# Narrow cross-attention: context and weights loaded in the normalization ahead of it, a second set of parts buffers, one block less up front, keys asked for in another order

## Chip, cores and metric

One core of one Trainium2 chip runs the whole program. The metric is the device time of one execution in microseconds (us), lower is better.

## What is computed

The reference is a two-layer perceiver: x is 4 batches x 256 queries x 256 features, the context 4 batches x 4096 keys x 256 features. It adds to x, one after the other: cross-attention with 16 heads of 64, self-attention, a gated mixture of 8 experts, cross-attention with 16 heads of 16 ("narrow"), differential self-attention, and a mixture of 32 experts. The change touches the narrow cross-attention and the normalization ahead of its query projection:

```
x = x + xattn(layernorm(x), ctx, ctx, lens)
# xattn: q = split(queries @ Wq); k = split(keys @ Wk); v = split(values @ Wv)     16 heads of 16
#        scores = q k^T / sqrt(16); scores = where(arange(4096) < lens, scores, -1e6)
#        out = softmax(scores) v;   return out @ Wo
```

## The kernel before

`perceiver` (L2627) runs one stage after the other. A stage is a `nc.Block()`: every engine has its own program in it, and no engine leaves before all of them have ended. For the narrow attention there are three such stages in a row: `normalize_and_transpose` (L59), `project_queries` (L147) and `narrow_attention` (L859).

**Narrow attention.** The context stands in DRAM (`ctx_split`) already split into a high and a low part, in 32 blocks (4 batches x CG = 8 blocks of 512 keys), 1 MB each. For a block n, TensorE (PE) projects keys, 2 x 6 matmuls of 512 columns into the banks `ps_s` (`project_keys`, L1080), and, for the blocks below 8, values, 2 halves x 12 matmuls of 256 columns (`project_values`, L1094), all of them with weights split into `w_high` and `w_low`. VectorE (DVE) masks the keys into `k_masked[m]` (`mask_keys`, L1278), ScalarE (ACT) copies them to `k_high[m]` (`take_high`, L1218), GpSimd (POOL) overwrites `k_masked[m]` by the low part (`take_low`, L1362), and SyncE's DMA queue (SP) stores both to the scratch rows `k_rows` in DRAM (`store_keys`, L985 and L987). ACT also copies the values out (`take_values`, L1228). m counts the two halves of the 256 features. There is one `k_masked` and one `k_high` for each m, so block n's mask waits for the landed store of block n-1.

Work then goes by pairs of heads, G = 32 of them, 8 to a batch. A pair's keys come back from `k_rows` and `edges` in 16 DMAs, 8 for either half of the keys (`load_keys`, L1000 and L1004), its queries in 6 (`load_queries`, L1014). First the row maximum is taken in ST = 16 units (`maximum`, L1112 on PE, `take_maximum`, L1291 on DVE, two banks in turn), turned and put into q (`turn_maximum` L1120, `take_maximum` L1242 on ACT). Then come 16 steps of scores (L1132), exponents (L1236) and weighting with the values (L1146). During pair a the units of pair a+1 and the projection of one later block of keys (a + FIRST) and values (a + 8) are put in by hand.

**What comes before pair 0** ("the first batch"): FIRST = CG + 3 = 11 blocks of keys and 8 of values in a ring over four `ctx` buffers, with the 16 units of pair 0 spread over it (two at each block from 5 on, the last four behind it). The order on each engine is written out by hand; each queue is in order:

- SP: both weights (L1026), ctx 0, the constants (L1028 to L1032), ctx 1 to 3, two selectors (L1035, L1036), queries 0 and 1, edges 0; then for each block its four stores, the ctx four blocks on, edges at 2, 4, 6, and the keys of pair 0 at blocks 3 (first half) and 7 (second half); behind the ring ctx 11, the value ctx 8, and the keys of pair 1.
- PE waits for the selectors, `fixed` (DVE has cleared the bank `ps_o`), `q_fixed` and both weight splits before its first matmul. The halves of the values go to `ps_m[1]` and `ps_p` for n < 4, both to `ps_p` from n = 4 on.
- POOL: 52 semaphores of the stage are raised by one (`Scope.sem`), then memsets of the queries (L1375, L1370), the two `w_low` (L1381), a memset of `v_all` (L1383) for which ACT's first `take_high` waits, then `take_low`.
- DVE: memset of `ps_o` (L1315), two `w_high` (L1271), lens and ends, edges 0 (L1284), then the masks.

## Time and profile before

| | us |
|---|---|
| median of 3 runs (4218.68 to 4230.01) | 4223.78 |
| the profiled execution | 4229.75 |
| its span, first to last instruction | 4227.9 |
| experts' last DVE instruction to the normalization's first | 2593.55 to 2594.86 |
| first weight DMA of the narrow stage | 2626.01 |
| its first matmul | 2647.57 |
| first exponent of pair 0 | 2740.16 |
| maxima of pair 1 finished | 2774.55 |
| busy over the span | PE 88%, DVE 63%, ACT 58%, POOL 39% |

Times are microseconds from the span's start. In the timeline a row is: start, length, engine, line, operation, tile written <- tiles read, shape, number of instructions merged, and in brackets the engine's idle time ahead of it with what ended it. A matmul's end is modelled, so busy TensorE time overlaps from one row to the next. "SPq" rows are DMA issues: their length is the issue, not the transfer.

### The profile page before, as it was taken

The numbers are of one execution on the slowest core, as the hardware profiler recorded it, in microseconds if no ns is written. First come the engines' busy times: TensorE is split into PE (matmuls) and PEld (weight loads), VectorE is DVE, ScalarE is ACT, GpSimd is POOL, SyncE is SP. The second block draws the span as 40 slices with busy tenths as digits, with TensorE's granted clock in tenths as the row PEclk, the third lists the DMA queues.
The fourth block names the chain that finished last, engine by engine and source line by source line (L and its number), as shares of the span: only waits on it lengthen the run. The fifth ranks groups of instructions, "written<-read, shape, count | busy, mean of one in ns | idle before, by whom it ended". The sixth has DMA issues, their size and how long they took to land. (4 is left out here: it accounts for less than half of the span.)

```text
span 4227.9 us, 77561 instructions
## 1 busy us (share of the span) xinstructions
PE 3717.0 (88%) x28216; PEld 2620.7 (62%) x28216; DVE 2669.3 (63%) x3564; ACT 2458.3 (58%) x4550; POOL 1650.8 (39%) x1365
## 2 busy tenths in 40 slices
PE   5899999999999999999777895699999987767299
PEld 2677777777777777777454794555555543333298
DVE  4766666666666666666155412477877877457577
ACT  3577777777777777777424111266666666435165
POOL 1566666666666666666402201201111000014033
PEclk9999999999999999999788897899999999779599
DMA  5776777677767776665110384777887754000011
GB/s 194 274 251 245 252 255 256 244 252 259 248 242 260 256 246 225 231 223 203 62 34 8 141 320 154 243 162 178 177 166 178 154 81 66 19 11 1 15 48 43
DMA packets 236312, 727.25 MB, mean 172 GB/s; under 512 B 47884, under 2 KB 133132, under 8 KB 167052
## 3 DMA queue, kind: packets, MB, share of 16 engines
q1 hardware_dynamic: 233248, 713.89, 54.6%
q0 software_dynamic: 2688, 8.39, 0.6%
q8 instruction: 230, 3.77, 0.4%
q14 instruction: 146, 1.20, 0.1%
HBM read 627.80 MB, written 94.37 MB: 171 GB/s over the span
## 5 line engine op out<-in xcount | busy, mean ns | idle before, releaser
L752 POOL TENSOR_TENSOR wa_acc<-wa_acc,wa_probs 128x512 f32<-128x512 f32 x960 | 1246.9, 1299 | 526.6 <-ACT wa_probs L613 446.6
L677 DVE TENSOR_REDUCE wa_mx<-wa_ps_m 128x2 f32<-128x1024 f32 x512 | 626.8, 1224 | 484.6 <-PE wa_ps_m L488 484.4
L613 ACT ACTIVATE wa_probs<-wa_ps_s 128x512 f32<-128x512 f32 x1024 | 556.3, 596 | 528.0 <-PE wa_ps_s L534 522.7
L1291 DVE TENSOR_REDUCE na_mx<-na_ps_m 128x2 f32<-128x1024 f32 x512 | 613.6, 1220 | 196.3 <-PE na_ps_m L1112 192.8
L1236 ACT ACTIVATE na_probs<-na_ps_s 128x512 f32<-128x512 f32 x1024 | 556.0, 594 | 312.2 <-PE na_ps_s L1132 309.8
L605 ACT ACTIVATE wa_ps_s<-wa_m_wide 128x512 f32<-128x512 f32 x1024 | 575.7, 605 | 1.0
L510 PE MATMUL wa_ps_o<-wa_probs,wa_values 128*64 128x256 f32 x4096 | 507.5, 391 | 0.0
L449 PE MATMUL wa_ps_k<-wa_k_ctx,wa_w_k 128*128 128x512 f32 x1488 | 388.4, 396 | 0.0
L475 PE MATMUL wa_ps_v<-wa_w_v,wa_v_ctx 128*128 128x256 f32 x2880 | 382.5, 282 | 0.0
L534 PE MATMUL wa_ps_s<-wa_qh,wa_keys 128*128 128x256 f32 x2048 | 381.6, 309 | 0.0
L510 PEld LDWEIGHTS wa_ps_o<-wa_probs,wa_values 128*64 128x64 f32 x4096 | 275.0, 138 | 149.8 <-issue 7.7
L666 DVE TENSOR_TENSOR wa_keys<-wa_ps_k,wa_keys 64x512 fp32r<-64x512 f32 x512 | 352.9, 689 | 20.5 <-ACT wa_keys L588 4.5
L475 PEld LDWEIGHTS wa_ps_v<-wa_w_v,wa_v_ctx 128*128 128x128 f32 x2880 | 363.1, 191 | 2.4
L1132 PE MATMUL na_ps_s<-na_q,na_keys 52*128 52x256 f32 x2048 | 260.5, 333 | 85.8 <-ACT na_probs L1236 81.5
L1132 PEld LDWEIGHTS na_ps_s<-na_q,na_keys 52*128 52x128 f32 x2048 | 160.7, 190 | 282.4 <-ACT na_probs L1236 257.9
L534 PEld LDWEIGHTS wa_ps_s<-wa_qh,wa_keys 128*128 128x128 f32 x2048 | 275.9, 189 | 70.4 <-issue 0.4
L588 ACT ACTIVATE wa_keys<-wa_ps_k 64x512 fp32r<-64x512 f32 x512 | 300.9, 588 | 31.9 <-PE wa_ps_k L449 25.7
L1362 POOL TENSOR_TENSOR na_k_masked<-na_k_masked,na_k_high 128x512 fp32r<-128x512 f32 x64 | 83.7, 1310 | 592.1 <-ACT na_k_high L1218 591.9
L449 PEld LDWEIGHTS wa_ps_k<-wa_k_ctx,wa_w_k 128*128 128x128 f32 x1488 | 263.2, 189 | 43.8 <-issue 0.4
L1146 PE MATMUL na_ps_o<-na_probs,na_v_all 128*17 128x256 f32 x4096 | 280.1, 392 | 0.0
L488 PE MATMUL wa_ps_m<-wa_keys,wa_qh 64*128 64x512 f32 x1024 | 257.6, 500 | 4.8 <-DVE wa_mx L677 3.0
L673 DVE COPY wa_values<-wa_ps_v 128x512 f32<-128x512 f32 x256 | 177.2, 692 | 87.5 <-PE wa_ps_v L475 80.6
(341 smaller groups left out, 5394.1 us busy)
## 6 DMA issues: line engine op xcount, KB each, us to landing
wa_k_ctx<-ctx_split SPq DMA_DIRECT2D x248, 1024.0 KB, 5.1
wa_v_ctx<-ctx_split SPq DMA_DIRECT2D x120, 1024.0 KB, 5.8
na_ctx<-ctx_split SPq DMA_DIRECT2D x56, 1024.0 KB, 11.8
na_keys<-k_rows SPq DMA_DIRECT2D x384, 128.0 KB
ctx_split<-wa_stage SPq DMA_DIRECT2D x32, 1024.0 KB, 9.2
wa_land<-in_ctxT SPq DMA_DIRECT2D x32, 512.0 KB, 10.1
ge_w_b<-in_w_rows SPq DMA_DIRECT2D x8, 2048.0 KB
k_rows<-na_k_high SPq DMA_DIRECT2D x64, 256.0 KB, 3.0
```

What stands on the lines that cost most here:

```text
L449: ins = pe.matmul(ps_k[:, :], w_k[g % 2][:, part, c, :], source[:, of, c, :], start=(n == 0), stop=(n == 3 * KD - 1))
L475: ins = pe.matmul(ps_v[:, i * 256:(i + 1) * 256], source[:, of, c, cols], w_v[:, part, c, :], start=(n == 0), stop=(n == 3 * KD - 1))
L510: ins = pe.matmul(ps_o[h * DH:(h + 1) * DH, 0:SQ], values[:, c, col:col + DH], probs[:, c % R, h * SQ:(h + 1) * SQ], start=(c == 0), stop= ...
L534: ins = pe.matmul(ps_s[(n + h) % BANKS][:, i * SQ:(i + 1) * SQ], keys[a % 2][h][:, (c + i) * P:(c + i + 1) * P], qh[a % 3][:, h, :], start ...
L605: act.activation(ps_s[n % BANKS][:, :].rearrange("p (c n) -> p c n", c=2), of_head, ACT.Copy).then_inc(init_done, 1)
L613: act.activation(probs[:, c % R:c % R + 2, h * SQ:(h + 1) * SQ], ps_s[n % BANKS][:, :].rearrange("p (c n) -> p c n", c=2), ACT.Exp).then_i ...
L666: dve.tensor_tensor(keys[g % 2][h][lo, cols], ps_k[hi, :], keys[g % 2][h][hi, cols].bitcast(F32), ALU.subtract).then_inc(kl_ready, 1)
L677: dve.tensor_reduce(mx[:, half, :, k], ps_m[:, :, :], AX.X, ALU.max).then_inc(m_taken, 1)
L752: pool.tensor_tensor(acc[:, :], acc[:, :], probs[:, c % R, :], ALU.add).then_inc(summed, 1)
L1132: ins = pe.matmul(ps_s[h][:, i * SQ:(i + 1) * SQ], keys[a % 3][r, (2 * t + i) * P:(2 * t + i + 1) * P], q[a % 3][r, :], start=True, stop=True)
L1236: act.activation(probs[:, c % RP:c % RP + 2, h * SQ:(h + 1) * SQ], ps_s[h][:, :].rearrange("p (c n) -> p c n", c=2), ACT.Exp).then_inc(exp ...
L1291: dve.tensor_reduce(mx[:, half, :, k], ps_m[n % 2][:, :, :], AX.X, ALU.max).then_inc(m_taken, 1)
```

## The change

1. The four `ctx` buffers, `probs` and the landing place of the weights (rows 0 and 1 of `probs`) are allocated around all three stages. The normalization's SP program loads both weights and ctx 0 to 3, and waits for them at its end. `narrow_attention` no longer loads them.
2. AHEAD goes from 3 to 2: 10 blocks before pair 0, and one key block more within the pairs.
3. Blocks with an even number below FIRST use `probs[2..5]` as `k_masked` and `k_high`, so a block's mask, high copy and low part wait for block n-2; the store semaphores are split by parity.
4. The first half of the values goes to the bank `ps_o`, which is no longer cleared, the second to `ps_p`, for all 8 blocks.
5. SP: constants and edge index first, no selectors or queries ahead of the ring (they go behind the stores of blocks 0 and 1); keys (pair, half) at block 4: (0, 0), 6: (1, 0), 8: (0, 1), and (1, 1) behind the ring, ahead of the ctx loads.
6. PE's waits for the selectors and the queries move to their first use. The units of pair 0: two at block 5, three at 6, three at 7, three at 9, five behind the ring.
7. POOL makes the two `w_low` ahead of the query memsets.

```diff
@@ normalize_and_transpose(..., ahead=None)
+        if ahead is not None:
+            ctx, ctx_split, w_land, sources = ahead
+            ahead_in = s.sem("ahead_in")
+            @block.sync
+            def _(sp):
+                for j, src in enumerate(sources):
+                    sp.dma_start(w_land[:, j, :, :], src.rearrange("(k p) n -> p k n", p=P)).then_inc(ahead_in, 16)
+                for n in range(4):
+                    sp.dma_start(ctx[n]..., ctx_split[n * P:(n + 1) * P, :]).then_inc(ahead_in, 16)
+                sp.wait_ge(ahead_in, 96)
@@ narrow_attention
-    AHEAD = 3
+    AHEAD = 2
+        first_masked = [probs[:, 2 + m, :] for m in range(2)]
+        first_high = [probs[:, 4 + m, :].bitcast(F32R) for m in range(2)]
-        loads, count = {}, [0] * 4
+        loads, count = {}, [-1] * 4
-        def first_bank(n, half):
-            return ps_m[1][:, 0, :] if half == 0 and n < 4 else ps_p
+        first_values = ps_o[:, :, :].rearrange("p a n -> p (a n)")
+        def first_bank(half):
+            return ps_p if half else first_values
+        FIRST_UNITS = {5: (0, 1), 6: (2, 3, 4), 7: (5, 6, 7), 9: (8, 9, 10)}
+        REST_UNITS = range(11, ST)
+        def masked_of(n, m):
+            return first_masked[m] if n < FIRST and n % 2 == 0 else k_masked[m][:, :]
+        def reused(n):
+            return n - 2 if 2 <= n < FIRST else n - 1 if n >= FIRST else None
@@ SP
-            for j, src in enumerate((w_k, w_v)):
-                sp.dma_start(w_land[:, j, :, :], ...).then_inc(w_in, 16)
-            load_ctx(0, False)
...
-            for n in range(1, 4):
-                load_ctx(n, False)
-            sp.dma_start(sel_num[:, :], consts["sel_num"]).then_inc(sel_in, 16)
-            sp.dma_start(sel_den[:, :], consts["sel_den"]).then_inc(sel_in, 16)
-            sp.wait_ge(q_fixed, 1 + 6)
-            load_queries(0)
-            load_queries(1)
             store_edges(0)
             for n in range(FIRST):
                 store_keys(n, 0)
                 store_keys(n, 1)
                 if n + 4 < FIRST:
                     load_ctx(n + 4, False)
+                if n == 0:
+                    sp.wait_ge(q_fixed, 1 + 6)
+                    load_queries(0)
+                if n == 1:
+                    load_queries(1)
+                    (sel_num and sel_den)
                 if n in (2, 4, 6):
                     store_edges(n // 2)
-                if n == 3 or n == 7:
-                    load_keys(0, n // 4)
+                if n == 4:
+                    load_keys(0, 0)
+                if n == 6:
+                    load_keys(1, 0)
+                if n == 8:
+                    load_keys(0, 1)
+            load_keys(1, 1)
             load_ctx(FIRST, False)
             load_ctx(CG, True)
-            load_keys(1, 0)
-            load_keys(1, 1)
@@ PE
-            pe.wait_ge(sel_in, 1 + 32)
-            pe.wait_ge(fixed, 1 + 1)
-            pe.wait_ge(q_fixed, 1 + 6)
             pe.wait_ge(high_split, 1 + 2)
             pe.wait_ge(low_split, 1 + 2)
...
-                    pe.wait_ge(v_ready, 1 + (2 * n + half if n >= 4 else max(2 * n + half - 1, 0)))
-                    project_values(n, half, first_bank(n, half))
+                    pe.wait_ge(v_ready, 1 + max(2 * n + half - 1, 0))
+                    project_values(n, half, first_bank(half))
@@ ACT, before pair 0
+            for m in range(2):
+                act.wait_ge(hi_stored[m][0], 1 + 16 * (FIRST // 2))
+                act.wait_ge(lo_stored[m][0], 1 + 16 * (FIRST // 2))
@@ DVE, mask_keys
-                dve.wait_ge(hi_ready, 1 + max(2 * (n - 1) + m + 1, 0))
-                dve.wait_ge(lo_stored[m], 1 + 16 * n)
+                if reused(n) is not None:
+                    dve.wait_ge(lo_stored[m][reused(n) % 2], 1 + 16 * (reused(n) // 2 + 1))
+                    dve.wait_ge(hi_ready, 1 + 2 * reused(n) + m + 1)
@@ DVE, start
-            dve.memset(ps_o[:, :, :], 0.0).then_inc(fixed, 1)
-            dve.wait_ge(w_in, 1 + 32)
@@ POOL: the two w_low now ahead of the memsets of q
+            for j in range(2):
+                pool.wait_ge(high_split, 1 + j + 1)
+                pool.tensor_tensor(w_low[:, j, :, :], w_land[:, j, :, :], w_high[:, j, :, :].bitcast(F32), ALU.subtract
+                                   ).then_inc(low_split, 1)
+            pool.wait_ge(low_split, 1 + 2)
             for i in range(3):
                 for h in range(2):
                     pool.memset(q[i]..., 1.0).then_inc(q_fixed, 1)
```

## Rows read from the trace of the kernel before

**Rows 1.** Waits from 2626 to 2765: engine, line, releaser, total, times, longest

```profile
PE na_ps_s L1080 <- DMA na_sel_den<-in_sel_den: 26.6, 1, 26.6
DVE na_k_masked L1278 <- DMA k_rows<-na_k_masked: 26.3, 11, 10.7
...
PE na_ps_p L1094 <- ACT na_v_all L1228: 10.5, 4, 4.8
```

**Rows 2.** Busy time by stretch: PE, PEld, DVE, ACT, POOL; clock share, DMA share, GB/s

```profile
2594.80:2607.50 12.70, 4.38 (x16) 2.43 (x16) 8.59 (x30) 4.56 (x10) 0.00 (x0) 0.50 0.00 1
...
2626.00:2647.50 21.50, 0.00 (x0) 0.00 (x0) 4.68 (x10) 0.00 (x0) 7.07 (x15) 0.50 0.76 249
2638.00:2643.00 5.00, 0.00 (x0) 0.00 (x0) 3.38 (x7) 0.00 (x0) 0.15 (x1) 0.50 0.97 393
...
2676.40:2727.70 51.30, 37.93 (x179) 29.94 (x178) 23.87 (x25) 12.14 (x20) 15.21 (x12) 0.83 0.78 242
...
2680.70:2685.00 4.30, 4.25 (x16) 3.96 (x17) 0.00 (x0) 0.60 (x1) 0.87 (x1) 0.50 0.96 133
```

**Rows 3.** Timeline around the start of the narrow stage, all engines

```profile
2606.65 0.81 ACT L143 ACTIVATE x_xT<-x_norm_pt 128x256 f32<-128x256 f32 x2 [0.42 <-PE x_norm_pt L133]
...
2626.01 0.39 SPq L1026 DMA_DIRECT2D na_probs<-in_L_xattn_Wk  x1
...
2629.48 0.76 DVE L1271 CAST na_w_high<-na_probs 128x512 fp32r<-128x512 f32 x2 [2.80 <-DMA na_probs<-in_L_xattn_Wv]
...
2630.38 2.09 POOL L1375 MEMSET na_q<- 4x256 f32 x6 [39.01 <-issue]
...
2634.72 2.48 POOL L1381 TENSOR_TENSOR na_w_low<-na_probs,na_w_high 128x512 fp32r<-128x512 f32 x2
```

**Rows 4.** TensorE's timeline: first rows of blocks, and of units of the maximum

```profile
2647.57 1.22 PE L1080 MATMUL na_ps_s<-na_ctx,na_w_high 128*128 128x512 f32 x2 [26.57 <-DMA na_sel_den<-in_sel_den]
...
2654.94 0.63 PE L1080 MATMUL na_ps_s<-na_ctx,na_w_high 128*128 128x512 f32 x2
...
2660.56 0.63 PE L1080 MATMUL na_ps_s<-na_ctx,na_w_high 128*128 128x512 f32 x2
...
2680.75 0.58 PE L1094 MATMUL na_ps_p<-na_w_high,na_ctx 128*128 128x256 f32 x1 [4.29 <-ACT na_v_all L1228]
...
2713.01 0.74 PE L1080 MATMUL na_ps_s<-na_ctx,na_w_high 128*128 128x512 f32 x2
...
2721.26 0.74 PE L1112 MATMUL na_ps_m<-na_keys,na_q 52*128 52x512 f32 x4 [1.58 <-DMA na_keys<-k_rows]
...
2747.02 0.79 PE L1112 MATMUL na_ps_m<-na_keys,na_q 52*128 52x512 f32 x2 [7.12 <-DMA na_keys<-k_rows]
```

**Rows 5.** SP's timeline near the end of the ring: issues of stores and keys

```profile
2712.70 0.26 SPq L1000 DMA_DIRECT2D na_keys<-edges  x1
...
2714.92 1.23 SPq L1004 DMA_DIRECT2D na_keys<-k_rows  x3
...
2719.21 0.32 SPq L987 DMA_DIRECT2D k_rows<-na_k_masked  x1
...
2733.01 0.29 SPq L1000 DMA_DIRECT2D na_keys<-edges  x1
```

**Rows 6.** Timelines of DVE and ACT: last units of pair 0, first exponent

```profile
2729.46 6.87 DVE L1291 TENSOR_REDUCE na_mx<-na_ps_m 128x2 f32<-128x1024 f32 x6
...
2740.16 1.08 ACT L1236 ACTIVATE na_probs<-na_ps_s 128x512 f32<-128x512 f32 x2
```

**Rows 7.** DVE's timeline: end of the maxima, pairs with and without a key block

```profile
2774.55 0.19 DVE L1295 TENSOR_REDUCE na_mrow<-na_mx 128x4 f32<-128x32 f32 x1
2803.48 0.18 DVE L1295 TENSOR_REDUCE na_mrow<-na_mx 128x4 f32<-128x32 f32 x1
...
3353.42 0.19 DVE L1295 TENSOR_REDUCE na_mrow<-na_mx 128x4 f32<-128x32 f32 x1
...
3382.09 0.19 DVE L1295 TENSOR_REDUCE na_mrow<-na_mx 128x4 f32<-128x32 f32 x1
```

More of the change, by code:

```diff
@@ L56, in sem, with normalize_and_transpose @@
         return handle
-def normalize_and_transpose(nc, name, x, xT, ident, affine=None, twice=False, rows=None):
+def normalize_and_transpose(nc, name, x, xT, ident, affine=None, twice=False, rows=None, ahead=None):
     with nc.cleanup_on_exit(), ExitStack() as stack:
@@ L856, in _, with narrow_attention @@
                                          ALU.mult, ALU.add).then_inc(added, 1)
-def narrow_attention(nc, ctx_split, w_k, w_v, lens, q_high, q_low, k_rows, edges, o_out, ident, consts):
+def narrow_attention(nc, ctx_split, ctx, probs, lens, q_high, q_low, k_rows, edges, o_out, ident, consts):
     DH = 16
@@ L994, in load_keys @@
                     sp.wait_ge(s_ready, 1 + (a - 2) * CH)
-                sp.wait_ge(hi_stored[m], 1 + 16 * (b * CG + (half + 1) * (CG // 2)))
-                sp.wait_ge(lo_stored[m], 1 + 16 * (b * CG + (half + 1) * (CG // 2)))
+                for parity in range(2):
+                    sp.wait_ge(hi_stored[m][parity], 1 + 16 * (b * CG + (half + 1) * (CG // 2)) // 2)
+                    sp.wait_ge(lo_stored[m][parity], 1 + 16 * (b * CG + (half + 1) * (CG // 2)) // 2)
                 sp.wait_ge(edge_stored, 1 + 16 * (b + 1))
@@ L1275, in mask_keys @@
                 dve.wait_ge(kp_done, 1 + 2 * n + m + 1)
-                dve.wait_ge(hi_ready, 1 + max(2 * (n - 1) + m + 1, 0))
-                dve.wait_ge(lo_stored[m], 1 + 16 * n)
-                dve.scalar_tensor_tensor(k_masked[m][:, :], key_index[:, :], ends[:, b, k:k + 1], bank[:, :],
+                if reused(n) is not None:
+                    dve.wait_ge(lo_stored[m][reused(n) % 2], 1 + 16 * (reused(n) // 2 + 1))
+                    dve.wait_ge(hi_ready, 1 + 2 * reused(n) + m + 1)
+                dve.scalar_tensor_tensor(masked_of(n, m), key_index[:, :], ends[:, b, k:k + 1], bank[:, :],
                                          ALU.is_lt, ALU.mult).then_inc(masked, 1)
@@ L1378, in _ @@
                 clear_shift(a)
-            for j in range(2):
-                pool.wait_ge(high_split, 1 + j + 1)
-                pool.tensor_tensor(w_low[:, j, :, :], w_land[:, j, :, :], w_high[:, j, :, :].bitcast(F32), ALU.subtract
-                                   ).then_inc(low_split, 1)
             pool.memset(v_all[0][:, :, :, DH:VW], 1.0).then_inc(ones_ready, 1)
@@ L2655, in _, with queries @@
                 sp.wait_ge(loaded, 48)
-        def queries(name, w, inner, scale, high, low, affine=None):
+        def queries(name, w, inner, scale, high, low, affine=None, ahead=None):
             with ExitStack() as inner_stack:
                 xT = Scope(nc, inner_stack, name).sb("xT", [P, KD, TOK])
-                normalize_and_transpose(nc, name + "_norm", x, xT, ident, affine, affine is not None)
+                normalize_and_transpose(nc, name + "_norm", x, xT, ident, affine, affine is not None, ahead=ahead)
                 project_queries(nc, name + "_proj", w, xT, inner, scale, high, low)
@@ L2694, in perceiver @@
                           a["w12_rows"], a["w3_rows"], x_slots0, y_slots0, x, ident, ones)
-        queries("x1", a["L1_xattn_Wq"], D, 0.25, q_high1, q_low1)
-        narrow_attention(nc, ctx_split, a["L1_xattn_Wk"], a["L1_xattn_Wv"], a["_lenS2"], q_high1, q_low1, k_rows1, edges1,
-                         oT1, ident, a)
+        with ExitStack() as inner_stack:
+            inner = Scope(nc, inner_stack, "np")
+            ctx = [inner.sb(f"ctx{i}", [P, 2, KD, 512], F32R) for i in range(4)]
+            probs = inner.sb("probs", [P, 12, 2 * SQ])
+            w_land = probs[:, 0:2, :].rearrange("p c (k n) -> p c k n", k=KD)
+            queries("x1", a["L1_xattn_Wq"], D, 0.25, q_high1, q_low1, ahead=(ctx, ctx_split, w_land, (a["L1_xattn_Wk"], a["L1_xattn_Wv"])))
+            narrow_attention(nc, ctx_split, ctx, probs, a["_lenS2"], q_high1, q_low1, k_rows1, edges1, oT1, ident, a)
         project_out(nc, "x1_out", oT1, D, a["L1_xattn_Wo"], x)
```

48 lines of the change are left out of this document (26 added, 22 removed).

## The prediction

> **What bounds it now.** I read the waits between 2626 and 2765 us first, then the busy time by stretch, then the timelines engine by engine. The chain that the page follows back from the last instruction covers only the end of the program, so the limits of this stage come from its own waits.
>
> The stage has three stretches. *Head*: from SP's first DMA (2626.01) to the first matmul (2647.57), PE stands still for 21.5 us, the longest wait of the stage, until a selector's DMA lands [rows 1, 3, 4]. That DMA is queued behind four context blocks of 1 MB, and the queue is busy for 0.76 of this time [rows 2]. During the normalization, 12.7 us, the DMA share is 0.00 [rows 2]. *Ring*: 2647.57 to the first exponent at 2740.16, 92.6 us. A block takes 5.62 us when PE is not held up (2654.94 to 2660.56) [rows 4]. From the fifth block on it is held up: DVE's masks wait 26.3 us in all for stores of the block before, ACT stands behind them, and PE waits 10.5 us for a value bank that ACT has yet to empty [rows 1]. *Pair 0*: after its first scores PE waits another 7.12 us for pair 1's keys [rows 4]. After that the pairs run in a steady beat of 28.93 us [rows 7].
>
> **Step 1, the loads in the normalization.** That block now ends when ACT's last copy ends, 2606.65 + 0.81 = 2607.46 [rows 3], and DVE begins it at 2594.86; SP should issue some 0.2 us ahead of DVE, as it did at 2626.01. From the first weight issue to DVE's first use of both weights went 3.47 us [rows 3]. Four context blocks are 4.19 MB, at the 393 GB/s of 2638 to 2643 [rows 2] 10.7 us. The loads end at 2594.7 + 3.5 + 10.7 = 2608.9, 1.4 us after ACT: the block grows by **1.4 us**. Bounds: nothing, and 7.6 us at the 249 GB/s that the whole head averaged; I take the first, because the slow average contains small constants, and here only large blocks are queued.
>
> The Trainium skill (DMA: Bandwidth & Descriptors, Rules for kernel authors) says to issue a DMA early, compute, and wait for it late. The change issues early but waits at the end of the same block, ahead of a query projection of 18 us that needs none of it. By that rule the 1.4 us are given away needlessly, and the sum below would be larger by them. The same page's Specifications put a core's share of HBM at some 358 GB/s; by that figure the loads take 11.7 us and the sum is 1 us smaller. The row's 393 GB/s is above the page's figure, and I go by the row.
>
> **Step 2, the head.** PE now needs only the two weight splits. DVE's are done early, since the weights are there. POOL's first instruction came at 2630.38, after it had raised 52 semaphores [rows 3]; with 54 it comes some 0.2 later, and the two w_low take 2.48 us [rows 3]. With 0.3 to the first matmul that is 2633.4, and with step 1 2634.8, against 2647.57: **gain 12.8 us** with the loss of step 1 in it. Bounds 6.6 (step 1's upper end) and 14.2. What is late next: constants and edge index no longer queue behind a context block. SP issues the last of them near 2629 and at the weights' 3.5 us they are there near 2633, with 2 to 3 us of DVE work before the first mask, due 3 us after the first matmul. The query memsets, now behind w_low, let ACT's first copy start about 1.5 us late, which the second value bank covers; without that cover it costs 1.5.
>
> **Step 3, the ring up to block 8.** Now 2713.01 - 2647.57 = 65.4 us [rows 4]. After it: eight blocks at 5.62 are 45.0; the first runs at half clock and takes 2654.94 - 2647.57 = 7.4, 1.8 more [rows 4]. Eight units of the maximum: two cost PE 0.74 [rows 4], and the third of a group of three must wait for DVE, 6.87 / 6 = 1.15 a unit [rows 6], so 0.7 + 1.9 + 1.9 = 4.5. The masks now wait for a store two blocks back, 11.2 us; I cost these waits at nothing. Values no longer share one bank, so PE no longer follows ACT: nothing either. The cover of both is that the queue keeps up; the third rival prices its loss.
>
> The new wait is for keys (0, 0), asked for at block 4 and used behind block 5. Let U be the start of block 4. In block 8 the last store was issued at 2719.21, 6.2 us after the block's start [rows 4, 5]. Then come 0.3 for its issue, 0.4 for ctx 8, 0.3 for the edges, and eight key issues in 3.45 us (2712.70 to 2716.15) [rows 5], so U + 10.7. The keys landed 2721.26 - 2716.15 = 5.1 us after their last issue [rows 4, 5]; here a context block is ahead, 1.05 MB at 393 GB/s or 2.7 us. They are there at U + 18.5. PE comes at U + 11.2 and waits 7.3 us. After a wait of 4.29 us matmuls ran at the 1.2 GHz level for 4.3 us and more [rows 2, 4], which costs about half of that, 2.2. Sum: 45.0 + 1.8 + 4.5 + 7.3 + 2.2 = 60.8, a **gain of 4.6 us**. Bounds: 14 without the wait and its clock; -2 if the keys take the 14 us from first issue to use that pair 1's took (2733.01 to 2747.02) [rows 4, 5].
>
> **Step 4, from block 8 to the first exponent.** Now 2740.16 - 2713.01 = 27.15 [rows 4, 6]. After it: block 8 has its last store issued at T + 6.5, keys (0, 1) issued by T + 10.0, landed by T + 15.1 with the 5.1 above. PE has long finished block 9 (T + 5.4). Eight units are left behind that wait: 0.8 for the first on PE at the low level [rows 4], 8 x 1.15 = 9.2 on DVE, then the 3.83 us from the last unit's end (2736.33) to 2740.16 for final reduction, turn, q and table load [rows 6]. T + 28.9: **loss 1.8 us**. One block less up front buys nothing here, since it went beside the same wait. Bounds: gain 7 if the keys land with block 9, loss 6 if they take 14 us.
>
> **Step 5, pair 1's keys.** Both halves are on their way before the first exponent, the second some 15 us before. PE's 7.12 us go: **gain 7.1**. Bounds 4 and 7.4. DVE's sixteen units of pair 1 are late next, and they already fill pair 0 in the trace, so no more comes.
>
> **Step 6, one key block more in the pairs.** Pairs with a key block take 28.93 us, the first without one 3382.09 - 3353.42 = 28.67 [rows 7]: **loss 0.3**. Upper bound 1.
>
> **Sum.** 12.8 + 4.6 - 1.8 + 7.1 - 0.3 = 22.4 us, 0.5%. The profiled execution took 4229.75 us, so 4207.4 by it. It lies 6 us above the median of the runs, so the forecast is 4223.8 - 22.4 = **4201.4 us**. A measurement of this kernel can tell about 0.3%, 12.7 us, from no change.
>
> **Rivals.**
> 1. *The key waits are shorter.* Rows for keys asked for while few stores are under way do not exist. If both waits vanish, steps 3 and 4 give 14 and 7 in place of 4.6 and -1.8: 41 us in all; if half of each does, 32, 4192. Against it: every key load seen took 8 us or more from first issue to use. Chance 0.15.
> 2. *The normalization waits for its DMAs.* At 249 GB/s step 1 costs 6.2 more: a gain of 16, 4208. Chance 0.10.
> 3. *The ring is bound by bytes.* From the first store to the landing of keys (0, 1) the queue moves nine blocks of stores (9.4 MB), six context blocks (6.3) and three key halves (2.5), 18.2 MB. At the 242 GB/s of 2676.4 to 2727.7 [rows 2] that is 75 us, plus 4.5 to the first store and 13.8 of units and turn behind it: 93.5 against 92.6 now. Steps 3 and 4 then give -1 together, the sum is 18.6, 4205. With rival 2 too it is 12, no measurable change. For it: in that stretch the DMA share is 0.78 although engines waited for each other. Against: the waits that thinned its use are what the change removes. Chance 0.12.
> 4. *The stages are moved and not shortened*: the loads cost the normalization what the head saves, or the key waits take back the rest. Under 12.7 us, 4215. Chance 0.07.
> 5. *Slower: the clock.* The change puts two waits of 7 and 9 us into the ring, between blocks that each pause at the hand-overs. If PE stays at the 1.2 GHz level afterwards, a block takes twice its 5.62 us. Every block at that level takes 5.6 back; four cancel the gain, seven make the kernel 0.3% slower, all eight give 4201 + 45 - 4 = 4242 (less the 4 that the sum already holds for the clock). Against it: PE returned to full clock within 5 us each time and has more unbroken work than before. Chance 0.03.
>
> The forecast itself has 0.53: gains of 15 to 30 us. **Range 4187 to 4214**: it reaches into rival 1 above the likeliest sum and takes in rivals 2 and 3. Faster by over 0.3%: forecast, rivals 1, 2 and most of 3, 0.87; within 0.3%: rival 4 and the overlap of 2 and 3, 0.10; slower 0.03.
>
> **What would show it.** The normalization's last instruction at about 2607.5 and the projection's weight DMA at 2609.5; first narrow matmul near 2634.8; blocks 0 to 4 in a beat of 5.6 us with no store wait of DVE above 1 us; one wait of PE for keys behind block 5 of 5 to 9 us and one behind block 9 of 8 to 10; first exponent near 2724.5; no wait for keys in pair 0; the steady beat unchanged at 28.9. I am wrong if the projection starts after 2613, if masks still wait for stores, or if a maximum waits for keys much longer than this.

## The result, and the profile after

| | us |
|---|---|
| before, median of 12 runs | 4225.38 (4218.68 to 4236.60) |
| after, median of 12 runs | 4218.38 (4208.27 to 4223.90) |
| ratio | 0.998, 95% interval 0.9971 to 0.999 |
| forecast | 4201.4 (4187 to 4214), a gain of 22.4 |

The change gains some 8.5 us (0.002 x 4225.38; the interval is 4 to 12), not quite four tenths of the forecast, and less than the 0.3% named there. The time lies outside the range. The profiled execution of after took 4209.71 us, 20 less than before's, but less than half of that is the change's, as the landmarks show. They are counted from the first instruction of the normalization, so that what happens upstream is out of them:

| us | before | after | forecast of the step |
|---|---|---|---|
| projection's weight DMA | 13.29 | 16.57 | +1.4, measured +3.3 |
| first narrow matmul | 52.71 | 41.75 | -12.8, measured -11.0 |
| first matmul to first exponent | 92.59 | 100.57 | -2.8, measured **+8.0** |
| first exponent to end of pair 1's maxima | 34.39 | 27.61 | -7.1, measured -6.8 |
| from there to pair 31's maxima | 859.86 | 861.04 | +0.3, measured +1.2 |
| from there to the last output | 46.72 | 38.75 | none, measured -8.0 |

The second row holds the first one in it. The rows from the second down to pair 31's maxima sum to a gain of 8.6 us, beside the 8.5 of the timed ratio. The last row is TensorE's clock in the last pair, whose code the change leaves alone (below).

**The normalization and the head of after**, from three timelines (start, us, engine; in brackets the idle time before and its releaser) and from the busy time by stretch (columns as in [rows 2]):

```profile
2593.49 0.40 SPq L97 DMA_DIRECT2D np_probs<-in_L_xattn_Wk  x1
...
2610.12 0.38 SPq L184 DMA_DIRECT2D x_proj_wq<-in_L_xattn_Wq  x1
...
2628.20 0.76 DVE L1305 CAST na_w_high<-np_probs 128x512 fp32r<-128x512 f32 x2 [3.01 <-PEq L165]
...
2632.72 2.48 POOL L1407 TENSOR_TENSOR na_w_low<-np_probs,na_w_high 128x512 fp32r<-128x512 f32 x2 [42.70 <-issue]
...
2635.30 1.19 PE L1110 MATMUL na_ps_s<-np_ctx,na_w_high 128*128 128x512 f32 x2 [12.12 <-POOL na_w_low L1407]
```

```profile
2593.50:2609.50 16.00, 4.38 (x16) 2.42 (x16) 8.58 (x30) 4.56 (x10) 0.00 (x0) 0.50 0.79 295
...
2600.00:2604.00 4.00, 2.80 (x11) 1.75 (x12) 3.02 (x11) 1.53 (x4) 0.00 (x0) 0.50 0.94 383
2604.00:2608.00 4.00, 1.58 (x7) 0.67 (x5) 0.00 (x0) 1.53 (x4) 0.00 (x0) 0.50 0.94 397
```

The DMA share of the normalization goes from 0.00 [rows 2] to 0.79. The selector's DMA no longer ends PE's longest wait [rows 4]; POOL's low parts do, as forecast. They begin only 4.6 us after the stage's first DMA (2632.72 - 2628.16); what stands ahead of them in POOL's program is the raising of its semaphores.

**The ring of after**, PE's timeline where it was held up, DVE's and SP's beside it:

```profile
2669.27 0.73 PE L1110 MATMUL na_ps_s<-np_ctx,na_w_high 128*128 128x512 f32 x2 [3.61 <-DVE np_probs L1313]
...
2676.47 0.28 PE L1124 MATMUL na_ps_p<-na_w_high,np_ctx 128*128 128x256 f32 x1
2685.82 1.22 PE L1144 MATMUL na_ps_m<-na_keys,na_q 52*128 52x512 f32 x4 [9.07 <-DMA na_keys<-k_rows]
...
2720.95 1.22 PE L1144 MATMUL na_ps_m<-na_keys,na_q 52*128 52x512 f32 x4 [10.31 <-DMA na_keys<-k_rows]
```

```profile
2666.16 2.40 DVE L1319 TENSOR_SCALAR na_v_all<-na_v_all,na_edge_ends,na_edge_rows 4x4096 fp32r<-4x4096 f32 x1 [8.20 <-DMA edges<-na_v_all]
```

```profile
2660.15 0.36 SPq L1049 DMA_DIRECT2D edges<-na_v_all  x1
...
2672.52 0.35 SPq L1016 DMA_DIRECT2D k_rows<-np_probs  x1
...
2673.96 0.26 SPq L1030 DMA_DIRECT2D na_keys<-edges  x1
2674.26 2.46 SPq L1034 DMA_DIRECT2D na_keys<-k_rows  x3
...
2677.13 1.23 SPq L1034 DMA_DIRECT2D na_keys<-k_rows  x3
```

The busy time by stretch of after, the first with the blocks in flow, the second with the wait for keys, the third around the second such wait:

```profile
2645.00:2665.00 20.00, 20.00 (x133) 18.38 (x132) 6.92 (x7) 7.39 (x12) 10.70 (x7) 1.00 0.97 310
2665.00:2685.00 20.00, 8.14 (x42) 6.79 (x40) 7.61 (x6) 4.70 (x8) 5.10 (x4) 0.81 0.97 306
...
2713.00:2736.00 23.00, 8.24 (x30) 3.34 (x30) 10.70 (x12) 2.16 (x4) 1.37 (x2) 0.54 1.04 219
```

PE is busy without a gap for 20 us at full clock. Then come three waits up to the first exponent, 23.0 us in all (3.61, 9.07 and 10.31), where before had 10.5 behind ACT [rows 1] and 1.58 for keys [rows 4]. The DMA share is 0.97 over these 40 us, where it was 0.78 in before [rows 2]. PE's waits for value banks and DVE's for stores are no longer among the thirty largest. The 7.12 us of pair 0 [rows 4] are gone.

### The profile page after: what moved, and what is told of

Same layout as the page of the kernel before. It is cut to its first block and busy times, and to the rows that moved or that the text cites. A ratio compares the mean times of both kernels' runs of the same rounds, so it can differ in the third digit from the quotient of the medians.

```text
span 4207.6 us, 77622 instructions
## 1 busy us (share of the span) xinstructions
PE 3706.7 (88%) x28216; PEld 2618.9 (62%) x28216; DVE 2668.6 (63%) x3563; ACT 2456.5 (58%) x4550; POOL 1652.3 (39%) x1365
## 5 line engine op out<-in xcount | busy, mean ns | idle before, releaser
L1267 ACT ACTIVATE np_probs<-na_ps_s 128x512 f32<-128x512 f32 x1024 | 555.8, 595 | 297.2 <-PE na_ps_s L1164 294.9
L680 DVE TENSOR_TENSOR wa_keys<-wa_ps_k,wa_keys 64x512 fp32r<-64x512 f32 x512 | 352.3, 688 | 18.5 <-ACT wa_keys L602 2.5
L1394 POOL TENSOR_TENSOR na_k_masked<-na_k_masked,na_k_high 128x512 fp32r<-128x512 f32 x54 | 71.3, 1320 | 571.4 <-ACT na_k_high L1249 570.9
L1178 PE MATMUL na_ps_o<-np_probs,na_v_all 128*17 128x256 f32 x4096 | 273.9, 385 | 0.2 <-ACT np_probs L1267 0.2
L1144 PE MATMUL na_ps_m<-na_keys,na_q 52*128 52x512 f32 x1024 | 212.4, 411 | 33.1 <-DMA na_keys<-k_rows 19.4
```

The lines of the kernel that those rows point to most:

```text
L680: dve.tensor_tensor(keys[g % 2][h][lo, cols], ps_k[hi, :], keys[g % 2][h][hi, cols].bitcast(F32), ALU.subtract).then_inc(kl_ready, 1)
L1267: act.activation(probs[:, c % RP:c % RP + 2, h * SQ:(h + 1) * SQ], ps_s[h][:, :].rearrange("p (c n) -> p c n", c=2), ACT.Exp).then_inc(exp ...
```

## Experiments

All kernels but the last two in the table, before and after ran once. They are compared by landmarks of the profiled execution, not by their totals, in us from the normalization's first instruction. The head itself varies by 1.7 us (weight DMA to first matmul 23.5 to 25.2 in fifteen kernels with the same head), and the weight DMA comes at 15.8 to 17.3 in the sixteen kernels that load four context blocks ahead, so the column "to first exponent" is the distance from the first matmul. How far a repeat agrees shows in one case: the kernel with the filled last pair has after's code up to there, and differs by 0.5 to the first exponent and by 0.2 at pair 1's maxima.

| kernel | us | first matmul | to first exponent | pair 1's maxima | pair 31's |
|---|---|---|---|---|---|
| before | 4229.75 | 52.71 | 92.59 | 179.69 | 1039.55 |
| after | 4209.71 | 41.75 | 100.57 | 169.93 | 1030.97 |
| loads only | 4230.33 | 48.06 | 94.77 | 176.34 | 1041.12 |
| edges first | 4216.31 | 41.35 | 100.48 | 169.36 | 1034.67 |
| queries early | 4217.33 | 39.69 | 98.60 | 166.23 | 1031.21 |
| old key order | 4204.97 | 41.77 | 88.64 | 159.92 | 1020.77 |
| old key order, single parts | 4206.53 | 41.72 | 89.40 | 159.46 | 1024.32 |
| key half (0, 0) earlier | 4211.41 | 39.67 | 97.62 | 166.96 | 1027.53 |
| key half (0, 1) earlier | 4215.59 | 42.06 | 97.73 | 167.05 | 1027.71 |
| key half (1, 0) later | 4214.14 | 39.76 | 99.30 | 166.58 | 1031.93 |
| three orders together | 4203.80 | 39.50 | 85.69 | 155.57 | 1015.90 |
| and context later | 4204.42 | 41.26 | 85.64 | 155.51 | 1015.87 |
| and low parts on DVE | 4204.53 | 36.35 | 89.67 | 155.52 | 1015.83 |
| and three blocks ahead | 4203.75 | 38.30 | 85.18 | 154.64 | 1015.08 |
| and pair 1's keys first | 4197.05 | 39.87 | 87.56 | 153.05 | 1013.20 |
| and memsets behind block 1 | 4208.75 | 41.30 | 88.85 | 159.85 | 1020.24 |
| and memsets behind block 5 | 4207.33 | 41.53 | 89.06 | 160.06 | 1020.69 |
| after, last pair filled | 4201.27 | 41.72 | 101.02 | 170.15 | 1030.37 |
| best version | 4191.11 | 33.85 | 87.56 | 149.15 | 1014.31 |
| best, memsets behind block 1 | 4191.63 | 33.51 | 87.77 | 148.84 | 1013.64 |

A row that begins with "and" is the three orders together with that one addition.

From pair 1's to pair 31's maxima a run takes 860 to 861 or 865 us. In each of the seven runs with 865 one single step from one pair's maxima to the next, between pair 25's and pair 28's, took 32.5 to 32.6 us and not 27.7, at a mean granted clock of 0.79. The step from pair 25's to pair 26's in edges first and in after (busy time by stretch):

```profile
3455.83:3488.39 32.56, 26.02 (x242) 12.32 (x238) 22.26 (x22) 17.99 (x34) 0.61 (x2) 0.79 0.40 58
```

```profile
3458.15:3485.87 27.72, 20.78 (x242) 10.36 (x238) 21.96 (x22) 17.98 (x34) 0.61 (x2) 1.00 0.45 68
```

The same 242 matmuls took 4.8 us longer, so the higher level is TensorE's clock in one pair. Why it fell there in some runs is open, and verdicts go by pair 1's maxima.

**The loads alone.** The kernel before with the first part of the change only:

```diff
+            sp.wait_ge(ahead_in, 96)      # weights and ctx 0 to 3, in the normalization
...
-            dve.wait_ge(w_in, 1 + 32)
```

> The kernel before with part 1 of the change alone: both weights and ctx 0 to 3 are loaded in the normalization; order, buffers and key requests as before. Measured from the normalization's first DVE instruction, the first narrow matmul came at 52.7 us before and at 41.75 us with the whole change. Here POOL still clears the queries ahead of w_low (4.2 to 6.3 us): if the loads alone bring the head's gain, the first matmul comes at 46 to 48 us, and the ring to the first exponent stays at 92.6 us within 2, so the first exponent gains 5 to 7 us; pair 1's keys still cost 7 us behind it. Rival, the ring is bound by the bytes its queue moves and by nothing else: the ring shortens by the 3 MB that no longer stand in front of it.

The first matmul came 4.7 us earlier, at the upper end of what was expected. The ring took 2.2 us longer, so the first exponent gained 2.5 and not 5 to 7, and pair 1's maxima 3.4. The rival, a ring shorter by the bytes that no longer stand ahead of it, did not show. The rest of after's gain at the first matmul comes with the other parts of the change; PE's longest wait there is for POOL's low parts (18.5 us, behind the query memsets), where in before it was for the selector. In this kernel the old waits stand (the masks' for stores 28.5 us, PE's for values 11.7).

**Edges ahead of the context.**

```diff
                 store_keys(n, 1)
+                if n in (1, 3, 5):
+                    store_edges(n // 2 + 1)
...
-                if n in (2, 4, 6):
-                    store_edges(n // 2)
```

> The changed kernel with the stores of edges 1 to 3 issued right behind the stores of blocks 1, 3 and 5, ahead of the ctx load and the queries, instead of one block later. Theory A (order on SP's queue): edges 1 was issued at 2660.15, behind 14 small DMAs, landed 6 us later, held DVE 8.2 us in front of block 4's masks and PE 3.6 us; so here that wait is gone, PE comes to the maxima behind block 5 about 3.6 us earlier and keys (0, 0) are asked for earlier too; first matmul to block 8 takes 62 to 64 us instead of 69.6. Theory B (bytes through the queue): the wait for keys behind block 5 grows by what is saved, and the stretch stays at 68 to 70 us.

The wait for edges is gone, and nothing is gained (69.6 us up to block 8, as theory B had it): PE comes to the maximum earlier and waits for the same keys longer. PE's timeline, and SP's:

```profile
2684.42 1.22 PE L1144 MATMUL na_ps_m<-na_keys,na_q 52*128 52x512 f32 x4 [14.83 <-DMA na_keys<-k_rows]
```

```profile
2669.27 0.27 SPq L1030 DMA_DIRECT2D na_keys<-edges  x1
2669.57 4.02 SPq L1034 DMA_DIRECT2D na_keys<-k_rows  x3
2673.64 0.56 SPq L1030 DMA_DIRECT2D na_keys<-edges  x1
2674.24 1.24 SPq L1034 DMA_DIRECT2D na_keys<-k_rows  x3
```

9.07 became 14.83. SP came to the keys at 2669.27, 76.87 from the start against 80.41 in after, but needed 6.2 us to issue the eight, 4.02 of them for three (1.23 in [rows 5]), and they landed at 92.02 against 92.27.

**Queries and selectors early.** `load_queries(0)`, `load_queries(1)` and the two selectors go ahead of block 0's stores and not between the stores of blocks 0 and 1.

> The changed kernel with the 12 query loads and the two selectors issued ahead of the ring, while SP stands idle (no wait for the memsets, which write other partitions). Theory A: SP reaches the stores of blocks 1 and 2 and edges 1 some 5 us earlier, edges 1 lands near 26 us after the first matmul instead of 31, DVE's 8.2 us wait shrinks below 3 and PE has none there; first matmul to block 8 takes 62 to 64 us instead of 69.6, as with the edges moved. Theory B: 68 to 70 us.

The wait behind the edges shrinks to 1.94 us, the first one for keys stays at 10.10. Up to block 8 it took 67.5 us, which neither theory had. The way to the exponent is 2 us shorter, and pair 1's maxima come 3.7 earlier, 2 of which the head had already.

**The old key order.** In after's ring, the keys are asked for as before:

```diff
-                if n == 4:
-                    load_keys(0, 0)
-                if n == 6:
-                    load_keys(1, 0)
-                if n == 8:
-                    load_keys(0, 1)
-            load_keys(1, 1)
+                if n == 3 or n == 7:
+                    load_keys(0, n // 4)
             load_ctx(FIRST, False)
             load_ctx(CG, True)
+            load_keys(1, 0)
+            load_keys(1, 1)
```

> The changed kernel with the keys asked for as before the change: pair 0's at blocks 3 and 7, pair 1's behind the ring and behind two ctx loads. Theory A: the two waits for keys in the ring (9.1 and 10.3 us) shrink to 5 or less each, since each request is a block earlier, and the first exponent comes 5 to 10 us earlier; the 7 us wait for pair 1's keys comes back. Maxima of pair 1 finished within 3 us of the changed kernel's. Theory B: the waits in the ring keep their size.

This is the largest effect of the single steps, and larger than expected: 11.9 us less to the first exponent, 10.0 at pair 1's maxima (expected: within 3 of after's). The first wait for keys is gone, the second fell from 10.31 to 2.93, and pair 0 has a wait again (3.98), so the last stretch took 29.5 against 27.6.

**Single parts buffers on top.** `masked_of` and `high_of` give one set, `reused(n)` is n - 1.

> The changed kernel with keys asked for as before the change (pair 0's at blocks 3 and 7) and without the second set of parts buffers: every block's mask, high copy and low part wait for block n-1 again. That key order with two sets came to the first exponent 88.6 us after the first matmul. If the second set carries the ring's gain, the waits of DVE for stores come back (10 us each after blocks 4 and 5) and the stretch takes 93 to 98 us. Rival: with a full queue the masks wait for the same bytes either way, and it stays within 2 us of 88.6.

DVE waits 30.8 us for stores again (11 times, up to 7.8), the first exponent comes 0.8 us later from the first matmul, and pair 1's maxima end at 159.46 against 159.92, as the rival had it. With this key order the second set of parts buffers buys nothing that one pair of runs can show. That the queue's time stands behind DVE's waits is the rival's reading, which fits; with after's own key order, or the three orders, single buffers were not run. The bank for the values, the block less up front and the spread of the units were never run alone either. This kernel has them and took 89.4 us to the exponent; the loads alone, which lacks them and asks for queries and selectors early, took 94.8.

**The three requests one by one**, each in after: (pair, half) (0, 0) at block 3 and not 4; (0, 1) at 7 and not 8; (1, 0) behind the ring and not at 6. The old key order has one thing more, pair 1's keys behind the two context loads.

> The changed kernel with only the first half of pair 0's keys asked for at block 3 instead of block 4. With all key requests as before the change, the first exponent came 11.9 us earlier. If the wait behind block 5 (9.1 us) carries it, that wait falls below 4 us and the first exponent comes 5 to 6 us earlier; the wait behind block 9 stays at 10. Rival: the stretch behind it takes it back, within 2 us of 142.3.

> The changed kernel with only the second half of pair 0's keys asked for at block 7 instead of block 8. If the request's place decides, the wait behind block 9 (10.3 us) falls to 3 to 5 us and the first exponent comes 5 to 7 us earlier. Rival: pair 1's half, asked for at block 6 and moved at 150 GB/s, still stands in front of it, and the wait stays above 8.

> The changed kernel with only pair 1's first half asked for behind the ring instead of at block 6. It was the third thing moved. If its 0.8 MB in front of the second half costs, the wait behind block 9 shrinks by 2 to 4 us. Rival: it had long landed, the ring is unchanged within 1 us, and pair 0 gets longer by 1 to 2 us.

The wait that each was to shorten came to 1.63 (from 9.07), 7.12 and 10.36 us (both from 10.31): the first as expected, the second by less, the third not at all. At pair 1's maxima they gain 3.0, 2.9 and 3.4, 9.2 in sum, nearly the 10.0 of the old order. From the first matmul on, which takes the head's variation out, they gain 0.9, 3.2 and 1.4 of 10.0, and the rest would come only together. Which reading holds was not settled; by both, no single request is the cause. With (0, 0) early the time came back elsewhere: DVE stood 8.78 us for the edges in the next blocks and the second wait for keys was 10.58.

What one block costs the first keys shows in the queue from the first store to their landing, in after, with (0, 0) at block 3, and in the three orders together (busy time by stretch):

```profile
2643.40:2685.82 42.42, 29.75 (x181) 26.51 (x180) 14.92 (x13) 13.55 (x23) 17.36 (x12) 0.90 0.95 305
```

```profile
2639.61:2674.58 34.97, 28.80 (x177) 25.79 (x176) 13.03 (x12) 13.46 (x23) 17.38 (x12) 0.95 0.94 300
```

```profile
2642.21:2677.54 35.33, 27.22 (x179) 24.77 (x177) 16.59 (x13) 13.54 (x23) 21.36 (x12) 0.96 0.97 310
```

At nearly the same share and rate, 12.9 MB were moved in after against 10.5 and 11.0. The difference is about a block's stores and one context block, 2.1 MB, which stand ahead of the keys if they are asked for one block later, and it took 7 us.

**The three orders together** (edges first, queries early, old key order).

> The changed kernel with three orders on SP's queue put right together: queries and selectors ahead of the ring, edges 1 to 3 right behind the stores of blocks 1, 3 and 5, keys asked for as before the change. Theory A (order decides): the 3.9 us wait behind edges goes and the first exponent, 130.4 us after the normalization's start with the old key order alone, comes at 123 to 127. Theory B (bytes decide): only the 2 us of the earlier head show, 127 to 129.

Pair 1's maxima are done at 155.57, 14.4 us earlier than in after, and the first exponent comes at 125.19, as theory A had it. The waits for keys are 8.11 and 3.17 in the ring and 4.23 in pair 0.

**Variations of it.** Context blocks 7 to 9 asked for later; w_low on DVE behind w_high; three context blocks in the normalization; pair 1's first keys ahead of context 10, the second ahead of the value block.

> As the run before it, with context blocks 7, 8 and 9 asked for later: 7 behind the keys at block 3, 8 and 9 at blocks 5 and 6. The queue's share was 1.0 from the first store to the landing of the keys of pair 0 and fell to 0.2 to 0.7 behind it. Theory B (bytes ahead of the keys decide): 1 to 2 MB fewer stand ahead of the keys and stores, they land 3 to 6 us earlier and the first exponent comes 3 to 5 us earlier than in the run before. Theory A: no change within 1 us, or a wait for a context block.

> The changed kernel with the three orders put right, and both w_low computed on DVE right behind w_high instead of on POOL, whose first instruction comes 4.5 us after SP's because it raises 54 semaphores first. If POOL's start sets the first matmul, that comes 4 to 5 us earlier than 39.5 us after the normalization's start. The first store follows DVE's edges, the masks and ACT's wait for POOL's memsets and gains less, 2 to 4 us; where the queue is full from the first store on, the first exponent gains as much as the first store, 2 to 4 us. Rival: it gains nothing, because masks and ACT wait for constants and memsets that come no sooner.

> The changed kernel with the three orders put right, and ctx 3 loaded at the start of the narrow stage instead of in the normalization. The normalization has grown by 3.3 us with four blocks; 1.05 MB at the 393 GB/s of the head before is 2.7 us. If its length is set by the bytes, the projection's weight DMA is issued 2.5 to 3 us sooner (13.0 to 13.8 us after the start, 15.8 to 16.6 with four), and everything behind it as much. Rival: the growth is a fixed cost of waiting for DMAs, and it stays above 15.5.

> The changed kernel with the three orders put right, and behind the ring the first half of pair 1's keys ahead of the ctx loads. From the first exponent to pair 1's last maximum it took 30.4 us with the ctx loads first and 27.6 us with the keys asked for inside the ring. If 2 MB of context in front of them is what they wait for, it takes 27.5 to 28.5 us, and the first exponent stays where it was, near 125 us. Rival: it stays near 30.

Context later: nothing at the exponent or at pair 1's maxima. The first keys landed 33.7 us after the first store and not 35.3, with the queue at 271 GB/s and not 310, and the second wait for keys grew from 3.17 to 4.88. Low parts on DVE: the first matmul comes 3.2 us earlier (4.2 counted from the projection's weight DMA), pair 1's maxima are the same to 0.05, and the keys' wait grew to 9.87. So a gain at the first matmul is not yet one at the maxima. The first store came only 0.9 us earlier. Three blocks ahead: the projection begins at 14.41 and not 15.81, less of a gain than the bytes were to give (13.0 to 13.8) and more than the rival (15.5 or later), and 0.9 of it arrives. Pair 1's keys first: 2.5 us at the maxima; the stretch from the exponent on took 25.6 against 30.4, and the exponent itself came 2.2 later, which was not expected.

**The query memsets on POOL.** ACT's first copy waits for the v_all memset, which in after stands behind twelve query memsets:

```profile
2635.26 4.18 POOL L1412 MEMSET na_q<- 4x256 f32 x6
2639.49 2.11 POOL L1402 MEMSET na_q<- 2x256 f32 x6
2641.66 1.05 POOL L1416 MEMSET na_v_all<- 128x512 f32 x1
```

The mask was there at 2639.11 (2638.39 + 0.72 on DVE), the copy began at 2642.74, 3.6 us late. Two kernels put v_all's memset first and the queries' behind the low parts of block 1, or of block 5.

> c_order with POOL's twelve query memsets put behind the low parts of block 1, so that the memset that ACT waits for at its start (v_all) comes right behind w_low. In the changed kernel ACT's first copy began at 2642.74, although its mask was there at 2639.11, behind 4.18 + 2.11 us of query memsets; the first store was issued 49.85 us after the normalization's first instruction, 46.94 + some in c_order. Theory that the ring is bound by the queue from its first store on: the first store comes about 3 to 3.5 us earlier and first exponent and pair 1's maxima come earlier by 2 to 3.5 (first exponent at 122 to 123 instead of 125.19, maxima at 152 to 153.5 instead of 155.57). Rival, that PE's and DVE's order sets the ring and the first stores are covered: first exponent within 1 us of 125.19.

> As c_ones, with the query memsets put behind the low parts of block 5 instead of block 1. In c_ones they delayed the low parts of block 2 by 4 us, its stores and with them the requests for keys (0, 0) by 2.6 us, so that the first exponent came 5.0 us later than in c_order and the question was not answered. Here they fall into TensorE's wait for keys. If the time of the first store is a term of the ring, the keys of block 5 land 1 to 3 us earlier than in c_order (91.0) and the first exponent comes at 122 to 124.5 (125.19). If it is not, the first exponent stays within 1 us of 125.19. If it comes later than 126.5, something other than the first store's time sets the keys' landing.

In both, the forecast and its rival missed; what came is the last case of the second expectation, later than 126.5. The first store came 1.4 and 1.1 us earlier than in the three orders (3.2 against the first matmul), and the first exponent 5 us later. The 91.0 in the second expectation was misread: the keys there landed at 82.92, after a wait of 8.11. Here they landed at 86.98 and 88.05. They were asked for 2.6 us later, 1.8 to 2.0 of it from the head, and landed 10 to 11 us behind the last issue and not 8.4. From the first store to the keys' landing the queue moved about as much as in the three orders (11.3 MB against 11.0), but at a share of 0.92 and 278 and 273 GB/s and not 310. So storing earlier did not land the keys earlier; why the queue ran thinner stays open.

**The last pair.** In after, each step of the last pair gets two matmuls of 512 columns that nobody reads:

```diff
+                    if a == G - 1:
+                        for h in range(2):
+                            r = slice(h * HEAD, h * HEAD + ROWS)
+                            pe.matmul(ps_m[0][:, h, :], q[a % 3][r, 0:P], keys[a % 3][r, 0:512], start=True, stop=True)
```

> The changed kernel with 32 more matmuls of 512 columns in the last pair, two in each of its 16 steps, into a bank that nobody reads. In five of the six traces so far TensorE's clock fell to the 1.2 GHz level in the last pair, and from the last pair's maxima to its last output 38.7 to 46.7 us went by. If the clock level is what spreads the runs of one kernel over 13 to 18 us, here the clock stays at full, and that stretch takes 30 to 34 us although the pair has more to compute; the total is at the low end of the changed kernel's runs, 4200 to 4208. Rival: the clock falls in spite of the work, and the stretch is longer than 40.

The stretch from pair 31's maxima to the last output, in before, after and the filled kernel (busy time by stretch):

```profile
3634.41:3681.13 46.72, 35.01 (x268) 14.99 (x264) 5.27 (x8) 21.25 (x40) 0.00 (x0) 0.60 0.01 1
```

```profile
3624.52:3663.27 38.75, 25.78 (x268) 11.17 (x264) 5.27 (x8) 21.24 (x40) 0.00 (x0) 0.87 0.01 2
```

```profile
3618.76:3655.01 36.25, 26.16 (x300) 12.92 (x296) 5.27 (x8) 21.24 (x40) 0.00 (x0) 1.00 0.01 2
```

The same 268 matmuls took 46.72 us at a mean granted clock of 0.60 and 38.75 at 0.87; with 32 more it was 36.25 at 1.00. The clock stayed at full, as expected; the stretch was to take 30 to 34. The one run took 4201.27 us, below all twelve of after's (4208.27 to 4223.90). So of the 20 us between the two profiled executions 8 are the clock of the last pair.

**The best version**, the three orders with w_low on DVE, three blocks ahead, pair 1's keys first and the filled last pair; then the same with the query memsets behind block 1.

> All four together: the orders, w_low on DVE, ctx 3 in the narrow stage, pair 1's keys ahead of the ctx loads, and the 32 matmuls that fill the last pair. From the sums of the parts the maxima of pair 1 finish 14.4 + 2 to 4 + 2.5 + 2 us, some 22 us, ahead of the changed kernel, and the last pair takes 36.3 us at full clock instead of 38.7 to 46.7. Expected median 4186 to 4196 us, 0.7 to 0.9% below the kernel before. Rival: gains that overlap at the full queue, 4197 to 4203.

> c_best with the same move of the query memsets. By the queue theory up to 2 us below c_best's 4186, that is 4183 to 4186; by the rival the same 4186. Ratio to the kernel before 0.990 to 0.992.

Median 4185.97 of 5 runs (4183.23 to 4193.09) against 4221.60 of 9 of before: 0.9913, interval 0.9899 to 0.9928, 36.7 us less than before. Its last output is 35.7 us earlier than before's in the two profiled executions: 30.5 of it at pair 1's maxima, 10.5 in the last pair by the filling, less 5.3 in the pairs between, where it had the slow pair. Against after, pair 1's maxima are done 20.8 us earlier, of the 22 expected. With the memsets moved: 4189.13 of 4 runs, 0.9913 (0.989 to 0.9936), no difference that these runs show.

## Why the prediction was wrong

**Step 1, mis-sized: 3.3 us and not 1.4.** The 383 and 397 GB/s of its middle were met; but the first windows moved less (272 from 2596 to 2600), and SP left the block at 16.57. Bounds held. That bytes are at least part of it the three kernels with three blocks show (14.2 to 14.4, against 15.8 to 17.3 with four). The figure of some 358 GB/s for a core's share of HBM (the Trainium skill, DMA: Bandwidth & Descriptors, Specifications) is below both measured windows, so the measurement stands. The Trainium skill (DMA: Bandwidth & Descriptors, Rules for kernel authors) advises to wait for a DMA late. One block less to wait for agrees with it, but gave only 0.9 us at pair 1's maxima; a wait that lies fully behind the projection was not tried.

**Step 2, right.** Without step 1 the head gained 14.2 by forecast (12.8 + 1.4) and 14.2 measured (10.96 + 3.28). That they agree to 0.1 is luck, since the head varies by 1.7. But what was said to be covered, ACT's first copy 1.5 us late, was 3.6: the memsets took 4.18 + 2.11 us beside DVE where before they took 2.09 + 2.11. Moving them gained nothing: pair 1's maxima came 4.3 and 4.5 us later in the three orders, and the best version stayed the same.

**Step 3, the step that failed.** Forecast 60.8 us up to block 8, measured 69.6 (before: 65.4). The sentence that fell is "The cover of both is that the queue keeps up": the keys were costed as if only one context block stood ahead of them in the queue. Where the 8.8 us are (3.6 for the edges, 1.8 more for the keys, 1.7 for the clock, 1.1 for the units), with U the start of block 4, 66.33:

- *The wait for edges, 3.6 us, costed at nothing.* Their store was issued at 2660.15, behind the queries, the selectors and a context block, and DVE went on at 2666.16. It stood 8.20 us, and with it block 4's masks, so its last store went out at U + 12.6 and not U + 6.2.
- *Keys at U + 25.9 and not U + 18.5.* Last issue at U + 18.5 (2678.36) and not U + 10.7; landing 7.5 us behind it, forecast 7.8. It looks as if the transfer was right and the request late, but with the edges out of the way SP came to the keys 3.5 us earlier, needed 6.2 us to issue them, and they landed at the same place (U + 26.2). Asked for one block earlier, with 2 MB less ahead of them, they landed 7 us sooner after the first store. So what stands ahead in the full queue sets the landing, and the edges' 3.6 us are time that PE would otherwise have stood for the keys. The wait of 9.1 (forecast 7.3) hides this: PE came to it at U + 16.9 and not U + 11.2.
- *The clock, 3.9 and not 2.2*: block 5 took 7.48 and block 6 7.62 in place of 5.62. Units cost 5.6 and not 4.5; some 0.6 is left over.

**Step 4**: 31.0, forecast 28.9, of the same kind: keys (0, 1) landed 16.1 us after block 8's start (127.40 - 111.35), forecast 15.1, and the tail was 14.9 and not 13.8. **Step 5**: right, 6.8 of 7.1. **Step 6**: 1.2, forecast 0.3, upper bound 1. Step 3 lies outside its own bound (-2, measured -4.2). The lower bound of step 4, a loss of 6, comes to 7 by its own terms; measured is 3.8.

**The rivals.** The third, that bytes bind the ring, was nearest and had 0.12: from the first store (2643.40) to the landing of keys (0, 1) (2720.95) went 77.6 us, by the rival 75. Its other terms were 8.1 and 14.9 against 4.5 and 13.8. Its picture of one steady rate of 242 GB/s did not hold, though. Up to the first keys the rate was 295 to 316 GB/s in the six kernels that ask at block 4; later, at a share of 1.04, it was 219 in after, and two kernels that began to store earlier landed their keys no earlier. What the runs showed is a queue that is full up to the first keys, and an order of requests in it that decides what lands first; the same requests in another order took 10 to 14 us off. The fourth rival (0.07), that the key waits take back the gain, is what the total looks like.

Against the fifth rival, the clock, stood that PE returned to full clock within 5 us each time. The trace of before does not bear that out. It stayed at the 1.2 GHz level for 30.7 us around the first exponent, and after did for 37.5:

```profile
2733.10:2763.80 30.70, 18.18 (x95) 8.99 (x95) 15.45 (x16) 9.63 (x17) 0.00 (x0) 0.50 1.01 225
```

```profile
2714.80:2752.30 37.50, 21.80 (x106) 10.23 (x107) 20.80 (x21) 9.55 (x17) 0.00 (x0) 0.50 1.01 216
```

PE was busy for less than six tenths of both, and what the level cost there was not separated.

So of what the change does, the loads and the new start of the stage gained 11 us at the first matmul and pair 1's keys 6.8. The second set of parts buffers gained nothing with the old key order, and asking for the first keys one block later (4 and 8 for 3 and 7), with pair 1's first half between them, lost about 10 net of what it gave pair 0. That the order did this is shown by the runs; how the 10 us divide among its requests is open.

## What to carry to other kernels

Before you cost a transfer at "issue plus landing time", ask whether the queue still has idle share once the waits in front are gone: here 0.78 became 0.97 and above, and then the issue itself stretches and every request costs those behind it. Count the bytes that stand ahead of a request: 2 MB took 7 us here. Order requests by who waits first, small stores that a wait hangs on ahead of big loads, and test an order as a whole, because a single move can hand the wait on. Compare stages by landmarks: the totals of two executions differed by 20 us where the change was worth 8.6.

## What the runs showed of the hardware that I had not expected

- The last pair's clock. In 17 traces without the filling the stretch took 38.75 to 46.72 us, in three with it 36.25 to 36.27. The code of the stretch is the same in the 17. Work that nobody reads saved 2.5 to 10.5 us, and without it the stretch varies by 8 us from one execution to another.
- A full share is not a full rate: with the three orders one window of 4 us moved 97 GB/s at a share of 0.93, another 381 at 1.07.
- Issue times on SP are not fixed: three key DMAs took 1.23, 2.46 and 4.02 us to issue.
- Six memsets of POOL took 4.18 us in after and 2.09 in before [rows 3].
